# Graph layers on one core: edge attributes applied to the gathered features on VectorE, second linear maps moved behind the segment sums

## The reference

```
outA = wA * g0 * e0                       # 32 numbers
outB = wB * sum_d g1[d] * e1[d] / sqrt(3) # 32
outC = wC * g0 * e1[d]                    # 32 for each d
outD = wD * g1[d] * e0                    # 32 for each d
mA, mB, mC, mD = segment sums of these over the edges of each destination node
c0 = mA @ W_l2_A0 + mB @ W_l2_B0 ;  c1[d] = mC[d] @ W_l2_C1 + mD[d] @ W_l2_D1
angle = 0.1 * (mA @ W_l3_A + mB @ W_l3_B) * node_vec1 / 8
result = layernorm(x + cos(angle) * self part + sin(angle) * (c0, c1))
```

## Time and profile before

| what | value |
|---|---|
| median of three runs | 5270.04 us |
| profiled execution, its own time (given as its span only) | 6176.2 us |
| PE busy (matmul) | 3676.8 us, 60% |
| DVE busy | 2879.2 us, 47% |
| ACT busy | 2789.4 us, 45% |
| POOL busy | 4072.2 us, 66% |
| gather stage, first gather issued to last | 3251.3 to 6099.2 us |
| mean granted TensorE clock | 0.695 of full speed |

### The profile page before, as it was taken

How to read it: one execution, slowest core, us unless ns; L and a number is a source line. 1 busy time by engine, 2 the same in 40 slices (tenths; PEclk the granted TensorE clock), 3 DMA queues, 4 the chain that set the end, 5 groups by cost and what they waited for, 6 DMA issues and landing times. The chain is left out here.

```text
span 6176.2 us, 86140 instructions
## 1 busy us (share of the span) xinstructions
PE 3676.8 (60%) x18515; PEld 3020.3 (49%) x18515; DVE 2879.2 (47%) x12091; ACT 2789.4 (45%) x9367; POOL 4072.2 (66%) x3270
## 2 busy tenths in 40 slices
PE   5555555555555555555474667665676666676666
PEld 3333434434333443433254566655565656666655
DVE  6565565556556555655471233333333333333334
ACT  2222222222222222222264567665665766676666
POOL 4888888888888888888745455544554545555552
PEclk7766666666776666667686666677666677766676
DMA  8666666666666666666772222222222222222221
GB/s 275 110 114 114 111 112 116 111 111 115 112 111 112 116 111 111 115 111 108 143 209 66 53 67 63 60 62 56 62 66 58 64 59 64 66 64 59 65 61 43
DMA packets 703023, 587.38 MB, mean 95 GB/s; under 512 B 287194, under 2 KB 572431, under 8 KB 701430
## 3 DMA queue, kind: packets, MB, share of 16 engines
q0 software_dynamic: 285872, 224.40, 26.2%
q1 hardware_dynamic: 394090, 297.48, 17.4%
q10 hardware_dynamic: 23004, 64.87, 2.8%
HBM read 374.12 MB, written 212.29 MB: 95 GB/s over the span
## 5 line engine op out<-in xcount | busy, mean ns | idle before, releaser
L786 POOL DMA_INDIRECT sums_scratch<-vals,to_i x1564 | 2455.1, 1570 | 543.9 <-issue 361.4
L1115 POOL DMA_INDIRECT fg<-f_scratch,src_e x1564 | 1482.7, 948 | 1389.5 <-DMA src_e<-in_src 757.2
L1179 ACT ACTIVATE hot<-raw,e_s 128x40 f32<-128x40 f32 x6272 | 1447.7, 315 | 436.1 <-issue 339.4
L704 PE MATMUL ps_n<-same,hot 128*40 128x128 f32 x3136 | 695.5, 415 | 1317.7 <-issue 1314.7
L704 PEld LDWEIGHTS ps_n<-same,hot 128*40 128x40 f32 x3136 | 556.7, 184 | 1426.8 <-issue 1362.5
L1144 PE MATMUL ps_eu<-hot,prod 128*128 128x120 f32 x3136 | 901.8, 373 | 280.6 <-issue 279.6
L1305 DVE TENSOR_TENSOR prod<-ps_ew,fg 128x256 f32<-128x256 f32 x392 | 164.3, 419 | 1711.0 <-remote 1304.4
L1142 PE MATMUL ps_eu<-hot,prod 128*128 128x40 f32 x3136 | 619.5, 280 | 429.3 <-issue 410.5
L1142 PEld LDWEIGHTS ps_eu<-hot,prod 128*128 128x128 f32 x3136 | 635.6, 242 | 481.0 <-issue 468.8
L1144 PEld LDWEIGHTS ps_eu<-hot,prod 128*128 128x128 f32 x3136 | 627.3, 243 | 299.0 <-issue 298.7
L744 ACT COPY near<-ps_n 40x512 f32<-40x512 f32 x196 | 113.3, 578 | 1420.7 <-PE ps_n L704 931.6
(11 more groups left out here) (210 smaller groups left out, 4269.3 us busy)
## 6 DMA issues: line engine op xcount, KB each, us to landing
srow_s<-in_src SPq DMA_DIRECT2D x194, 512.0 KB
hid_scratch<-hid SPq DMA_DIRECT2D x196, 256.0 KB
hid_e<-hid_scratch SPq DMA_DIRECT2D x196, 256.0 KB
e_s<-in_edge_attr SPq DMA_DIRECT2D x194, 256.0 KB
sums_scratch<-zeros ACTq DMA_DIRECT2D x12, 2112.0 KB, 30.5
sums_scratch<-vals,to_i POOLq DMA_INDIRECT x1564
fg<-f_scratch,src_e POOLq DMA_INDIRECT x1564
t_in<-sums_scratch POOLq DMA_DIRECT2D x72, 256.0 KB, 8.1
```

What stands on the lines that cost most here:

```text
L704: last = pe.matmul(ps_n[t // TH][:, t % TH, :], hot[:, k, t, :], same[:, k, t, :], start=True, stop=True)
L786: pool.indirect_dma_start(out=sums_d[i], out_offset=bass.IndirectOffsetOnAxis(ap=to_i[:, j, t:t + 1], axis=0), in_=vals[:, j, t, :], in_of ...
L1115: pool.indirect_dma_start(out=fg[:, j, t, :], out_offset=None, in_=f_d, in_offset=bass.IndirectOffsetOnAxis(ap=src_s[:, j, t:t + 1], axis= ...
L1179: last = act.activation(hot[:, k, t, c, :], raw[:, k, t, :], ACT.Copy, scale=e4_s[:, j, t, c:c + 1])
```

## The change

- `hot` has one copy of the one-hot matrix (scaled by e0) instead of four: ACT issues 8 instructions a group instead of 32. The unscaled `raw` is used as the second one-hot matrix.
- DVE gets three new instructions a group, before the products: `vec` = the vector features times e1 (768 elements a partition, both inputs in SBUF), `spread[0:3]` = the scalar features times e1 (768, both inputs in SBUF), and a reduce over d of `vec` into `spread[3]` (768 in, 256 out). The products are again four (256, 768, 768, 256 elements): two take `fg`, two take `spread`.
- PE's segment sums are two matmuls of 40 columns a tile instead of one of 40 and one of 120. The second linear maps are no longer made per group; they are made per 256 finished nodes, in place of the transposes, with the angle's weights as a 129th column.
- ACT's five copies a group and DVE's `from_sums` go away. DVE adds the segment sums of group s-2 straight from `ps_eu`, ahead of its wait for the gathers.
- SP waits for the products of group s-4 where it waited for `fc2` of s-4. Late weights: 20 DMAs instead of 24.

```diff
@@ PE, gather stage
+                                done(pe, e_hot, m)
                                 done(pe, e_prod, m)
-                                done(pe, e_hot, m)
-                                done(pe, e_sums, m, 2)
+                                done(pe, e_add, m, 2)
                                 for t in range(TS):
                                     hf = t // TH
-                                    pe.matmul(ps_u[k][:, hf, 0, :], prod[:, k, t, 0, :], hot[:, k, t, 0, :],
+                                    pe.matmul(ps_u[k][:, hf, 0, :], prod[:, k, t, 0, :], hot[:, k, t, :],
-                                    last = pe.matmul(ps_u[k][:, hf, 1:4, :], prod[:, k, t, 1, :], hot[:, k, t, 1:4, :],
+                                    last = pe.matmul(ps_u[k][:, hf, 1, :], prod[:, k, t, 1, :], raw[:, k, t, :],
...
-                                    pe.transpose(ps_lin[:, c, :], staged[:, 0, c:HB:HC], ident[:, :])
...
+                                    for g in range(2):
+                                        last = pe.matmul(ps_lin[:, c, :], staged[:, g, c:HB:HC], lin_w[:, g, :],
+                                                         start=(g == 0), stop=(g == 1))
...
-                                for c in range(4):
-                                    pe.matmul(ps_c[k][:, 0, :, :], lin_w[:, c, :], sums[:, k, :, c, :], start=(c == 0), stop=(c == 3))
-                                last = pe.matmul(ps_c[k][:, 1, :, :], lin_w[:, 4, :], sums_a[:, k, :, :], start=True, stop=True)
@@ ACT
-                                    for c in range(4):
-                                        last = act.activation(hot[:, k, t, c, :], raw[:, k, t, :], ACT.Copy,
-                                                              scale=e4_s[:, j, t, c:c + 1])
+                                    last = act.activation(hot[:, k, t, :], raw[:, k, t, :], ACT.Copy,
+                                                          scale=e4_s[:, j, t, 0:1])
...
-                                for c in range(4):
-                                    act.copy(sums_a[MUL * c:MUL * (c + 1), i % 2, :, :], ps_u[i % 2][MUL * c:MUL * (c + 1), :, c, :])
-                                act.copy(sums[:, i % 2, :, :, :], ps_u[i % 2][:, :, :, :]).then_inc(e_sums, 1)
@@ DVE body
                                 done(dve, e_hot, s, 2)
+                                done(dve, e_seg, s, 2)
                                 dve.tensor_tensor(raw[:, k, :, :], ...
+                            m, r, i = at(s, q, j, 2)
+                            if live_sg(m):
...
+                                done(dve, e_seg, m)
+                                done(dve, e_add, m, 1)
+                                to = table[:, :, bass.ds(b0, W)]
+                                dve.tensor_tensor(to, ps_u[i % 2][:, 0, :, :], to, ALU.add).then_inc(e_add1, 1)
+                                done(dve, e_add1, m)
+                                to = table[:, :, bass.ds(b1, W)]
+                                dve.tensor_tensor(to, ps_u[i % 2][:, 1, :, :], to, ALU.add).then_inc(e_add, 1)
+                            if live_sg(s):
+                                uses(dve, e4_ld[j], q + 1, 16)
...
                                     uses(dve, gath[j], q + 1, 16 * TS)
+                                attrs = e4_s[:, j, :, 1:4, None].to_broadcast([P, TS, 3, MUL])
+                                done(dve, e_dot, s, 1)
+                                dve.tensor_tensor(vec[:, :, :, :], fg[:, j, :, MUL:D].rearrange("p t (d u) -> p t d u", d=3),
+                                                  attrs, ALU.mult).then_inc(e_vec, 1)
+                                done(dve, e_prod, s, 1)
+                                dve.tensor_tensor(spread[:, :, 0:3, :],
+                                                  fg[:, j, :, None, 0:MUL].to_broadcast([P, TS, 3, MUL]),
+                                                  attrs, ALU.mult).then_inc(e_dir, 1)
+                                done(dve, e_vec, s)
+                                dve.tensor_reduce(spread[:, :, 3, :], vec[:, :, :, :].rearrange("p t d u -> p t u d"),
+                                                  AX.X, ALU.add).then_inc(e_dot, 1)
+                                done(dve, e_fc2, s)
+                                dve.tensor_tensor(prod[:, k, :, 0, 0:MUL], ps_w[k][:, :, 0, :], fg[:, j, :, 0:MUL], ALU.mult)
+                                dve.tensor_tensor(prod[:, k, :, 0, MUL:D].rearrange("p t (d u) -> p t d u", d=3),
+                                                  ps_w[k][:, :, 2, None, :].to_broadcast([P, TS, 3, MUL]),
+                                                  fg[:, j, :, MUL:D].rearrange("p t (d u) -> p t d u", d=3), ALU.mult)
+                                done(dve, e_dir, s)
+                                dve.tensor_tensor(prod[:, k, :, 1, 0:3 * MUL].rearrange("p t (d u) -> p t d u", d=3),
+                                                  ps_w[k][:, :, 1, None, :].to_broadcast([P, TS, 3, MUL]),
+                                                  spread[:, :, 0:3, :], ALU.mult)
+                                done(dve, e_dot, s)
+                                dve.tensor_tensor(prod[:, k, :, 1, 3 * MUL:D], ps_w[k][:, :, 3, :],
+                                                  spread[:, :, 3, :], ALU.mult).then_inc(e_prod, 1)
@@ SP
-                            done(sp, e_fc2, s, UN)
+                            done(sp, e_prod, s, UN)
```

More of the change, by code:

```diff
@@ L586, in late_weights @@
                         def late_weights():
[L587 to L593, removed]
+                            dve.wait_ge(w_in, 16 * LATE)
+                            dve.tensor_scalar(lin_f[3 * MUL:D, 1, :], lin_f[3 * MUL:D, 1, :], 3.0 ** -0.5, None, ALU.mult)
                             dve.tensor_scalar(fc2_w[:, :], fc2_w[:, :], 1.0 / 8.0, None, ALU.mult).then_inc(w_scaled, 1)
@@ L1039, in graph_layers @@
             raw = tmp("raw", [P, 2, TS, W])
-            hot = tmp("hot1", [P, 2, TS, 4, W])
+            hot = tmp("hot1", [P, 2, TS, W])
+            vec = tmp("vec", [P, TS, 3, MUL])
+            spread = tmp("spread", [P, TS, 4, MUL])
             prod = tmp("prod", [P, 2, TS, 2, D])
-            sums = tmp("sums", [P, 2, 2, 4, W])
-            sums_a = tmp("sums_a", [P, 2, 2, W])
             ps_w = [bank(f"ps_ew{i}", [P, TS, 4, MUL], s4) for i in range(2)]
[L1045 to L1050, removed]
+            ps_u = [bank(f"ps_eu{i}", [P, 2, 2, W], s4) for i in range(2)]
+            ps_lin = bank("ps_lin", [NP, HC, D + 1], s4)
             staged = tmp("staged", [P, 2, HB])
-            lin = tmp("lin_g", [NP, HC, D])
             xs_in = tmp("xs_in", [NP, HC, 2, D])
@@ L1148, in body @@
                             if j == 2 and live_self(q - 2):
                                 done(pe, g_stage, q - 2)
-                                done(pe, e_add, m if live_sg(m) else NSG + i, 2)
-                                done(pe, g_lin, q - 2, 1)
+                                done(pe, g_y, q - 2, 1)
                                 for c in range(HC):
-                                    pe.transpose(ps_lin[:, c, :], staged[:, 0, c:HB:HC], ident[:, :])
-                                for c in range(HC):
-                                    last = pe.transpose(ps_ang[:, c:c + 1], staged[0:1, 1, c:HB:HC], ident[0:1, 0:1])
+                                    for g in range(2):
+                                        last = pe.matmul(ps_lin[:, c, :], staged[:, g, c:HB:HC], lin_w[:, g, :],
+                                                         start=(g == 0), stop=(g == 1))
@@ L1261, in combined @@
                             for c in range(HC):
-                                last = dve.scalar_tensor_tensor(out=y[:, c, :], in0=lin[:, c, :],
+                                last = dve.scalar_tensor_tensor(out=y[:, c, :], in0=ps_lin[:, c, 0:D],
                                                                 scalar=sin_a[:, c:c + 1], in1=t_sb[:, c, :],
@@ L1303, in body @@
                                     uses(dve, gath[j], q + 1, 16 * TS)
-                                for g in range(2):
-                                    dve.tensor_tensor(prod[:, k, :, g, 0:MUL], ps_w[k][:, :, g, :], fg[:, j, :, 0:MUL], ALU.mult)
-                                    last = dve.tensor_tensor(
-                                        prod[:, k, :, g, MUL:D].rearrange("p t (d u) -> p t d u", d=3),
-                                        ps_w[k][:, :, 2 + g, None, :].to_broadcast([P, TS, 3, MUL]),
-                                        fg[:, j, :, MUL:D].rearrange("p t (d u) -> p t d u", d=3), ALU.mult)
@@ L1310, in body @@
-                                last.then_inc(e_prod, 1)
-                            m, r, i = at(s, q, j, 3)
-                            if live_sg(m):
-                                b0 = dve.value_load(base_i[0:1, bass.ds(m * 2, 1)], min_val=0, max_val=N)
```

(13 more changed lines are left out.)

58 lines of the change are left out of this document (21 added, 37 removed).

## The result

The changed kernel takes 5345.99 us (median of four, 5345.46 to 5347.69) against 5270.45 before: ratio 1.0146, 95% interval 1.0134 to 1.0159. Forecast were 5367 us and a range of 5240 to 5430.

The account below looks back on a forecast made before the run. The prediction took POOL's gathers, about 9.98 us a group, to bound the gather stage: 5279 + 98 (holds) - 1 (tail) = 5376, and with the median 9 below that total, 5367 us. The range was 5240 to 5430.

Parts of the forecast that it names:

- The gather stage is bound by POOL's 1.248 us starts.: Gather stage, unprofiled: POOL starts a gather every 1.248 us, about 9.98 us a group, and sets the pace.
- The extra 906 us of the first profile are "a thing of the profiled execution".: Gather stage: PE's 934 us of "issue" stops make the profile's 906 us over the median and belong to the profiled execution.
- ACT and PE savings are worth 0: Gather stage: ACT falls from 9.36 to 2.7 us a group, PE from 12.6 to 8.1 at the lower clock; gain 0.
- DVE 7.5 us a group, hidden: Gather stage: DVE rises from 4.77 to 7.5 us busy a group, below POOL's 9.98, so it costs nothing.
- DVE will stand at its wait in nearly every body: Gather stage: DVE, even 9.6 us in its heaviest body, will be waiting for the gathers in nearly every body.
- Each group holds POOL for 0.5 us: Gather stage: `vec` and `spread` lengthen POOL's gathers by 0.5 us a group, between locked and random phase; 98 us in all.
- "An undisturbed gather passes some point 0.12 us after its start": POOL's gathers: a DVE instruction with two SBUF inputs running at that point holds the gather until the instruction ends.
- Tail -1 us: Behind the last gather: 2.7 us more on DVE, copies and maps gone; -1 us, between -5 and +5.
- DVE waiting for POOL, up to 0.94 us an instruction: Gather stage: by the Trainium skill's rule `vec` and `spread` could each wait up to 0.94 us, DVE reaching some 9.8 us a group.
- The rival built on it: DVE becomes the bound at 10.8 us a group, 5430 us; chance 0.11, including POOL held by both effects.
- The faster rival: Gather stage: ACT with PE, not POOL, set the unprofiled pace; 5215 us taken for a partial gain; chance 0.19.
- same: Gather stage: POOL bound, and the phase lets both `vec` and `spread` miss the gathers; 5270 us; chance 0.13.

Follow-up runs that it names:

- e1: Changed kernel with edge attributes copied into PSUM, where `vec` and `spread` read them, run with the stops; 6130.9 us against 6135.6 for the kernel before (ratio 0.998).
- r2: Kernel before plus two unused 768 element DVE instructions a group, both inputs in SBUF, run without stops; 5360.2 us, ratio 1.0183 to before.
- e6: Changed kernel with edge attributes (for `vec`, `spread`) and the node number row (for `raw`) read from PSUM; 5253.6 us, ratio 0.9981 to before.
- e4: Changed kernel with the first product moved between `vec` and `spread`, run with the stops; 6124.9 us, ratio 0.9968 to before.
- e7: Changed kernel with edge attributes read from PSUM, plus 24 ACT instructions a group writing to a spare tile; 5260.2 us, ratio 0.9998 to before.
- e5: Changed kernel without `vec`, `spread` and the reduce, the last two products reading `fg` (so another output); 5253.4 us, ratio 0.9986 to before.
- r3: Kernel before plus two unused 768 element DVE instructions a group, one input in SBUF, one in PSUM, run without stops; 5266.2 us, ratio 1.0007 to before.
- r1: Changed kernel with edge attributes copied into PSUM, where `vec` and `spread` read them, run without stops; 5252.9 us, ratio 0.998 to before.
- r4: Changed kernel with the first product moved between `vec` and `spread`, so `spread` starts 1.20 us behind `vec`, run without stops; 5298.9 us, ratio 1.0069 to before.

## Why the prediction was right

- *The gather stage is bound by POOL's 1.248 us starts.* Right. Span less holds is 5245 to 5253 us for every kernel tried, and 3251 + 1951 + 48 (tail) is 5250.
- *The extra 906 us of the first profile are "a thing of the profiled execution".* Wrong in its cause, though it gave the right base. Unprofiled runs can have them too (all twelve runs of e1, of which one was profiled, took 6105 to 6156 us), and the profiles without them span within 4 us of their kernel's median (5343.9 and 5346.0), r2's 18 us more. The stops come and go between sessions: e6 had none on the same chip on which e1 to e4 had them.
- *ACT and PE savings are worth 0.* Right to some microseconds (e7: 7, of which 5 by holds).
- *DVE 7.5 us a group, hidden.* 1456.6/196 = 7.4; hidden (e5). The reduce took 1.03 us for 0.95.
- *DVE will stand at its wait in nearly every body.* Wrong: in 106 groups of 196. The price left out is the register loads of the table's two addresses, which now stand between `raw` and the adds: 1.1 us a group (173.7 over 155) in which DVE waited for "issue". With it, starts of `vec` lie in many phases; that the loads are what spreads them was not tested. In the kernel before they stood behind the products and were covered; r3, which has them there, shows 2.6 us of such waits in all.
- *Each group holds POOL for 0.5 us.* 28 + 54 = 82 us under `vec` and `spread`, so 0.42 a group: the value reckoned for a random phase, not the mean I took with the locked one. That it is this value is in part luck, for the phases are not random: 43 of 196 `vec` start within 0.04 us ahead or 0.02 behind of a gather's start. This term is 16 us too large, and explains most of the 21 us between 5367 and 5346.
- *"An undisturbed gather passes some point 0.12 us after its start", where the instruction can hold it.* Wrong as stated, and not followed in the forecast's own sum: `vec`, put 0.06 us behind a gather's start, would still have been running at that gather's point and would have held it for some 0.9 us a group, where the sum has 0. The sum used the rule that the traces bear out: whether a gather is held is settled by who starts first (804 held, 285 not), and the 0.12 us are only what the wait doesn't cost, since a held gather needs 0.82 of its 0.94 us behind the end of the DVE instruction.
- *Tail -1 us.* It went from 54.0 (r3) to 47.5 us (5343.9 - 5296.4), -6. Together: 5270 + 82 - 6 = 5346. To the microsecond that is chance: the 5270 is 7 us above the kernel's later medians, and the sum leaves out that `raw` and `t_sb` held gathers for 12 us where the whole gather line had 6 in the first trace before.
- *DVE waiting for POOL, up to 0.94 us an instruction*, weighed against the earlier trace rows: it exists, but is at most some 0.06 us, and only for instructions that start together with a gather (0.97 to 1.02 us for 0.96; with one input in PSUM, in r1, e6 and r3, 0.956 at most at the same place). The rival built on it falls. The Trainium skill (SBUF — State Buffer, Who interferes with whom) has whoever issues first block the other for its whole instruction: that agrees with DVE's side, and not with POOL's, whose gather of 0.94 us delays `vec` by 0.06. Its statement that `tensor_reduce` never contends on trn2 agrees with the trace: none of 196 held a gather.
- *The faster rival* (ACT or PE as the true pace) falls with e7; *same* (a phase that misses) is what r4 reaches by half.

The direction and the size were forecast by the mechanism that was then found. The range of 5240 to 5430 was wide enough to hold no change as well, so its being met says little.

What the gather waits for inside the chip no run shows. The Trainium skill (SBUF — State Buffer, Who interferes with whom) says that such a VectorE instruction contends through the shared read interface with a GpSimd instruction that reads SBUF. That an indirect gather is one, by its indices, is not on the page, which even infers that `tensor_tensor` does not stall the DMAs of GpSimd; here it does, for 93.7 us, and the measurement decides. The runs show the condition: two SBUF inputs (or an SBUF to SBUF copy), begun ahead of the gather and still running behind its start.

## What to carry to other kernels

Before moving work onto an idle engine, look whether the engine that sets the pace changes its instruction lengths beside instructions of the new kind: `raw` showed here, with 6 us in total, the price that came to 82. Where POOL issues indirect DMAs on the critical path, give VectorE's long two-input instructions one input in PSUM; with the copy that this took, VectorE was busy for 1481 us of the stage instead of 1453, and nearly all of the price came back. And an engine that is not the bottleneck can lose half of its work without a gain: ACT's halving was worth some microseconds in 5270.

## What the runs showed of the hardware that was not expected

The stops. In some sessions PE stands idle between single instructions, with nothing to wait for that the profile shows; such waits of ACT and DVE grow too (ACT's `hot` 376 us in e1 against 150 in r1, DVE's longest at `table` 12.2 against 1.3). PE's timeline in e1:

```profile
4529.17 0.22 PE L1135 MATMUL ps_eu<-raw,prod 128*128 128x40 f32 x1 [2.50 <-issue]
4532.07 0.22 PE L1135 MATMUL ps_eu<-raw,prod 128*128 128x40 f32 x1 [2.68 <-issue]
4534.90 0.38 PE L1143 MATMUL ps_lin<-lin_w,staged 128*128 128x129 f32 x1 [2.60 <-issue]
4537.77 0.38 PE L1143 MATMUL ps_lin<-lin_w,staged 128*128 128x129 f32 x1 [2.49 <-issue]
```

They appear in the gather stage, spare the neighbour stage (first gather at 3244 to 3251 us with and without them), and cost each kernel alike: by the medians 812 to 881 us for the kernel before and for e1 to e4 against r1 to r4. What starves the engines stays open; no run was aimed at it.

Second, the hold is sharp and settled at the start: a DVE instruction that begins 0.044 us ahead of a gather holds it to its own end (r2), one that begins 0.042 us ahead doesn't hold it at all (r2), whatever is left of it. So the price depends on phase to hundredths of a microsecond, as r4 shows. That the gather needs the contested thing only for a moment at its start, and the DVE instruction for all its length, would fit both the 0.12 us and DVE's wait of at most 0.06; it is argued, not shown.
